# Gated projection weights built by GpSimd, products copied out by ScalarE, and a second LayerNorm in three groups

## What is computed

```
x = x + gate_msa[:, None, :] * _attention(_modulate(_layernorm(x), shift_msa, scale_msa), qkv_w, qkv_b, proj_w, proj_b)
x = x + gate_mlp[:, None, :] * _mlp(_modulate(_layernorm(x), shift_mlp, scale_mlp), fc1_w, fc1_b, fc2_w, fc2_b)
```

## Time and profile before

| | |
|---|---|
| median of 3 runs | 472.64 us |
| profiled execution, its own time | 472.34 us |
| its span (first to last instruction) | 470.6 us |
| TensorE busy | 429.0 us, 91% |
| VectorE busy | 287.5 us, 61% |
| ScalarE busy | 221.8 us, 47% |
| GpSimd busy | 89.2 us, 19% |
| mean granted TensorE clock | 0.964 of full speed |

### The profile page before, as it was taken

The page is one execution under the profiler, slowest core; times in us unless marked ns, Lnnn a source line. Parts: engine busy times, 40 slices in busy tenths (PEclk is TensorE's granted clock), DMA queues, the critical chain, the costliest instruction groups (busy, mean ns, idle before and its releaser), DMA issues.

```text
span 470.6 us, 11337 instructions
## 1 busy us (share of the span) xinstructions
PE 429.0 (91%) x4617; PEld 274.5 (58%) x4617; DVE 287.5 (61%) x808; ACT 221.8 (47%) x459; POOL 89.2 (19%) x108
## 2 busy tenths in 40 slices
PE   8999999999959999899968888877689999999987
PEld 4666655565636666666645665566434665656554
DVE  3698844576674644667737666567878555644422
ACT  3245533242037979687777677523256241421200
POOL 5059999950000000000000000013500000000000
PEclk9999999999979999899959899999969999999999
DMA  6996000000000000000000000000000000000011
GB/s 171 316 296 187 3 4 1 2 2 2 0 0 1 1 2 2 3 1 3 1 5 3 5 4 3 3 0 1 2 1 1 13 23 16 26 13 27 15 37 39
DMA packets 7785, 14.55 MB, mean 31 GB/s; under 512 B 2541, under 2 KB 6098, under 8 KB 7607
## 3 DMA queue, kind: packets, MB, share of 16 engines
q1 hardware_dynamic: 7732, 13.82, 9.8%
HBM read 11.37 MB, written 2.38 MB: 29 GB/s over the span
## 4 chain that ended last, share of the span: by engine, by line
PE 73%; DVE 12%; ACT 9%; issue 5%; ACTq 0%; DVEq 0%
PE psum L886 12%; PE psum L470 12%; PE psum L904 12%; PE psum L737 6%; PE psum L570 3%; DVE MX L1273 2%; PE psum L812 2%; PE psum L723 2%; ACT scratch L998 2%; PE psum L662 2%; PE psum L642 2%; ACT big L1030 2%; PE psum L582 2%; PE psum L687 2%; PE psum L526 1%
## 5 line engine op out<-in xcount | busy, mean ns | idle before, releaser
L886 PE MATMUL psum<-scratch,W 128*128 128x512 f16 (+1 forms) x252 | 60.9, 393 | 2.3 <-DVE scratch L1268 2.3
L470 PE MATMUL psum<-ident 128*128 128x320 f32 (+2 forms) x156 | 59.9, 472 | 0.0
L737 PE MATMUL psum<-WQ,scratch 128*128 128x288 f16 (+1 forms) x336 | 51.3, 297 | 5.0 <-DVE scratch L1279 5.0
L904 PE MATMUL psum<-W,big 128*128 128x288 f16 x432 | 55.7, 286 | 0.0
L464 POOL TENSOR_TENSOR X<-X,big 128x288 f32<-128x288 f32 x16 | 12.6, 794 | 225.4 <-DVE big L1388 224.2
L1108 ACT ACTIVATE big<-psum 128x512 f32<-128x512 f32 x36 | 21.5, 599 | 68.5 <-PE psum L886 68.4
L904 PEld LDWEIGHTS psum<-W,big 128*128 128x128 f16 x432 | 41.0, 98 | 13.7 <-issue 3.8
L1273 DVE TENSOR_REDUCE MX<-psum 128x8 f32<-128x1024 f32 x32 | 39.0, 1219 | 15.7 <-PE psum L687 15.2
L998 ACT ACTIVATE scratch<-psum,MOD 128x512 f32<-128x512 f32 (+3 forms) x48 | 34.2, 773 | 20.3 <-PE psum L662 7.3
L886 PEld LDWEIGHTS psum<-scratch,W 128*128 128x128 f16 (+1 forms) x252 | 25.3, 101 | 30.1 <-issue 3.7
L1412 DVE TENSOR_SCALAR big<-big 128x512 f16<-128x512 f32 x36 | 15.3, 424 | 44.1 <-ACT big L1108 44.0
(11 more groups left out here) (209 smaller groups left out, 767.3 us busy)
## 6 DMA issues: line engine op xcount, KB each, us to landing
X<-in_x_dram SPq DMA_DIRECT2D x4, 576.0 KB, 15.7
out_dram<-big SPq DMA_DIRECT2D x16, 144.0 KB, 1.7
big<-in_L_cond_W_dram SPq DMA_DIRECT2D x1, 2268.0 KB
big<-in_L_cond_ada_w_dram SPq DMA_DIRECT2D x2, 864.0 KB, 18.6
stage<-in_L_cond_fc_w_dram SPq DMA_DIRECT2D x1, 1296.0 KB
big<-in_L_cond_fc_w_dram SPq DMA_DIRECT2D x1, 1152.0 KB
stage<-in_L_cond_qkv_w_dram SPq DMA_DIRECT2D x1, 864.0 KB
big<-in_L_cond_fc_w_dram SPq DMA_DIRECT2D x3, 144.0 KB
```

The source lines that it names most:

```text
L470: pe.matmul(out[:, 0:cols], left, left[:, 0:1].broadcast_to([P, cols]), start=True, stop=True)
L737: mm = pe.matmul(UB[gu % 2][:, 0:D], HT[0:r, n % 2, a_, P * a:P * a + P], WQ[0:r, w_, D * w:D * w + D], start=(p_ == 0), stop=(p_ == 6))
L886: mm = pe.matmul(FB[idx % 3], W1[0:r, w_, P * m:P * m + P], HT[0:r, n % 2, a_, :], start=(p_ == 0), stop=(p_ == 6))
L904: mm = pe.matmul(YB[t % 2][:, 0:D], g[:, a_, f, cols], W2[:, w_, f, :], start=False, stop=(f == NF - 1 and w_ == 1))
```

## The change

1. GpSimd no longer prepares WP at the start. After its other preparations it waits for the attention gates and then, for each batch, multiplies the staged weights and bias by the gate and splits the product into halves (7 instructions per batch, semaphore `folded`). WP holds two batches. The attention gates go to GATE0, scaled by FINE.
2. ScalarE copies the projection's products out of PSUM (`product_out`), VectorE no longer does. The first PSUM bank of the three is bank 7 instead of bank 2.
3. The second LayerNorm is three groups: tiles 0 to 3, 4 to 7, 8 to 15. The variance step is a function of its own, `norm_var`. The first two groups' square roots lie among the projection's copies on ScalarE, the third in `gelu(9)` before m = 2. VectorE's statistics of tiles 8 to 11 lie in the first fc1 chunk, those of tiles 12 to 15 and `source(10)` in the second.
4. TensorE turns chunk 8 before it projects chunk 7, not after.

```diff
-        GATE = sb("GATE", [P, 2, B, D])
+        GATE = sb("GATE", [P, B, D])
...
-        QB = [bank[2], bank[5], bank[6]]
+        QB = [bank[7], bank[5], bank[6]]
...
-        NORMS = [(0, TPC * n, TPC) for n in range(NCH)] + [(1, 8 * b, 8) for b in range(B)]
+        NORMS = [(0, TPC * n, TPC) for n in range(NCH)] + [(1, 0, TPC), (1, TPC, TPC), (1, 8, 8)]
...
-            for src, dst, n, s_ in ((SWQ, WQ, 3 * D, in_wq), (SWP, WP, D, in_wp), (SW1, W1, MLP, in_w1)):
+            for src, dst, n, s_ in ((SWQ, WQ, 3 * D, in_wq), (SW1, W1, MLP, in_w1)):
...
+            pool.wait_ge(in_wp, 96)
+            pool.wait_ge(fill_done, FG + 3)
+            for b in range(B):
+                r = slice(0, 98)
+                chain(pool.tensor_tensor(WPG[:, 0:2, :], SWP[:, 0:2, :], GATE0[:, b, :].unsqueeze(1).broadcast_to([P, 2, D]), ALU.mult))
+                chain(pool.tensor_copy(WP[:, b, 0:2, :], WPG[:, 0:2, :]))
+                pool.tensor_tensor(WP[:, b, 2:4, :], WPG[:, 0:2, :], WP[:, b, 0:2, :], ALU.subtract).then_inc(folded, 1)
+                chain(pool.tensor_tensor(WPG[r, 2, :], SWP[r, 2, :], GATE0[r, b, :], ALU.mult))
+                chain(pool.tensor_copy(WP[r, b, 4, :], WPG[r, 2, :]))
+                chain(pool.tensor_scalar(WP[r, b, 4, :], WP[r, b, 4, :], lowrow[r, :], None, ALU.mult))
+                pool.tensor_tensor(WP[r, b, 4, :], WPG[r, 2, :], WP[r, b, 4, :], ALU.add).then_inc(folded, 1)
+                pool.wait_ge(folded, 2 * b + 2)
...
             turn(NCH)
             for n in range(NCH, 2 * NCH):
-                if n + 1 < 2 * NCH:
-                    turn(n + 1)
+                turn(n + 1)
                 project(n)
-            turn(2 * NCH)
...
+                    act.wait_ge(folded, 2 * B)
...
+            def product_out(t):
+                act.wait_ge(proj_ready, t + 1)
+                if t >= 6:
+                    act.wait_ge(x_mid, t - 5)
+                act.mul(YT[:, t % 6, :], QB[t % 3][:, 0:D], 1.0 / (FINE * FINE)).then_inc(proj_mul, 1)
+
             turn_out(NCH, None)
             for n in range(NCH, 2 * NCH):
-                if n + 1 < 2 * NCH:
-                    turn_out(n + 1, None)
-            norm_root(NCH)
-            turn_out(2 * NCH, 1)
-            norm_root(NCH + 1)
+                turn_out(n + 1, None if n + 1 < 2 * NCH else 1)
+                for j in range(TPC):
+                    product_out(TPC * (n - NCH) + j)
+                if n in (NCH + 1, NCH + 2):
+                    norm_root(n - 1)
...
+                    if n == 2 * NCH + 1 and m == 2:
+                        norm_root(NCH + 2)
...
+            def middle(t0, k):
+                for t in range(t0, t0 + k):
+                    dve.wait_ge(x_mid, t + 1)
+                    stat(1, t)
+
             split(NCH)
-            for n in range(NCH, 2 * NCH):
...
+            split(NCH + 1)
+            split(NCH + 2)
+            middle(0, TPC)
+            norm_var(NCH)
+            split(NCH + 3)
+            norm_scales(NCH)
+            source(2 * NCH, 1)
+            middle(TPC, TPC)
+            norm_var(NCH + 1)
             split(2 * NCH)
-            for t in range(NT - 3, NT):
-                dve.wait_ge(x_mid, t + 1)
-                stat(1, t)
+            norm_scales(NCH + 1)
             source(2 * NCH + 1, 1)
-            norm_scales(NCH + 1)
...
+                    if c_ == 1 and m == 2:
+                        norm_scales(NCH + 2)
+                        source(n + 1, 1)
...
+                    if c_ == 0 and m in FC2_AT:
+                        middle(8 + FC2_AT.index(m), 1)
+                    if c_ == 1 and m < 2:
+                        middle(12 + 2 * m, 2)
+                    if c_ == 1 and m == 1:
+                        norm_var(NCH + 2)
```

More of the change, by code:

```diff
@@ L53, in build @@
         o += 18 * D
+        SW1 = big[:, o:o + 12 * D].rearrange("p (b n) -> p b n", b=3)
+        o += 12 * D
+        assert 8192 + 2048 <= o - 3 * D and 12288 + 2 * D <= o
         SWP = big[:, o:o + 3 * D].rearrange("p (b n) -> p b n", b=3)
         o += 3 * D
-        SW1 = big[:, o:o + 12 * D].rearrange("p (b n) -> p b n", b=3)
-        o += 12 * D
+        WPG = big[:, WTILES * D:(WTILES + 3) * D].rearrange("p (b n) -> p b n", b=3)
+        GATE0 = big[:, 12288:12288 + B * D].rearrange("p (b n) -> p b n", b=B)
         JUNK = big[0:WROWS, o:o + 4 * D].rearrange("p (a n) -> p a n", a=4)
@@ L188, in build @@
         weights = sem("weights")
+        folded = sem("folded")
         mod_part = sem("mod_part")
@@ L856, in project @@
                 if n == NCH:
-                    pe.wait_ge(weights, 4)
+                    pe.wait_ge(folded, 2 * B)
                 for j in range(TPC):
@@ L862, in project @@
                     for p_, (a_, w_, r) in enumerate(PARTS):
-                        mm = pe.matmul(QB[t % 3][:, 0:D], HT[0:r, n % 2, a_, P * j:P * j + P], WP[0:r, w_, :], start=(p_ == 0), stop=(p_ == 6))
+                        mm = pe.matmul(QB[t % 3][:, 0:D], HT[0:r, n % 2, a_, P * j:P * j + P], WP[0:r, t // 8, w_, :], start=(p_ == 0), stop=(p_ == 6))
                     mm.then_inc(proj_ready, 1)
@@ L875, in fc1 @@
                 if n == 2 * NCH:
-                    pe.wait_ge(weights, 6)
+                    pe.wait_ge(weights, 4)
                 for m in range(NF):
@@ L893, in fc2 @@
                 if c_ == 0:
-                    pe.wait_ge(weights, 8)
+                    pe.wait_ge(weights, 6)
                 g = GT[c_ % 2]
@@ L921, in fill_out @@
                     g, b = divmod(n - FG - 1, 2)
-                    cp = act.mul(GATE[:, g, b, :], f[:, 0:D], 1.0 / (FINE * FINE))
+                    if n == FG + 1:
+                        act.wait_ge(weights, 4)
+                    cp = act.mul(GATE[:, b, :], f[:, 0:D], 1.0 / (FINE * FINE)) if g else act.mul(GATE0[:, b, :], f[:, 0:D], FINE)
                 elif work[n] == "P'":
@@ L1222, in stat, with norm_var @@
                 dve.bn_aggr(MV[:, l, t, :], BN[:, t % 2, :]).then_inc(bn_s, 1)
+            def norm_var(q):
+                l, t0, k = NORMS[q]
+                dve.wait_ge(bn_s, 2 * (NT * l + t0 + k))
+                dve.tensor_scalar(ST[:, l, 0, t0:t0 + k], MV[:, l, t0:t0 + k, 1], EPS, None, ALU.add).then_inc(stats, 1)
             def norm_scales(q):
@@ L1295, in _ @@
                 rotated(t)
+            norm_var(0)
             norm_scales(0)
@@ L1304, in _ @@
             ones_rows(0)
+            norm_var(1)
             norm_scales(1)
@@ L1342, in normalise @@
                 if w == 0:
-                    dve.wait_ge(weights, 8)
+                    dve.wait_ge(weights, 6)
                 for c_ in range(2):
```

26 lines of the change are left out of this document (5 added, 21 removed).

## The result

The changed kernel takes 475.30 us (475.38 as the median of all its 5 runs); the kernel before took 472.64 us beside it. The ratio is 1.0044, with a 95% interval of 1.0025 to 1.0062: slower by about 2.1 us, where I had forecast 1.1 us less. Times here are medians of the fast runs; of every kernel, the one before included, other executions are 6 to 16 us longer, and a few of those that count as fast lie about 5 us above the rest, which widens the intervals. Measured again as `again`, the changed kernel took 476.25 us beside 472.70 for the kernel before, 3.6 us more (ratio 1.0089, 1.0041 to 1.0137).

A forecast was written before the change was run, and what follows sets the result against it. TensorE, busy nine tenths and carrying the chain for most of the span, was taken as the bound. fc1's earlier start -2.86, clock 0, fc1(9) wait +1.7 gave -1.1 us: 471.5, stated as 471.4, range 468.4 to 474.5.

The forecast's parts named there:

- The fold: GpSimd's gate multiplication during QKV, about 145 to 159 us: covered, taken as 0, bounds 0 to 1.65 us.
- Products to ScalarE: In the projection, sixteen ScalarE copies of 0.41 us add nothing, and TensorE's 1.20 us pause goes.
- turn(7): Third block waits for the Sqrt table load and root: a 2.4 us pause, block 1.0 us later than before.
- VectorE's own line: From the block's split through norm_scales(4), 1.0 us, and source(8), 1.44, chunk 8 is ready at 332.6 us.
- The third block of turn(8): ScalarE takes the second root before turn_out(8), so TensorE pauses a new 3.35 us, 333.55 to 336.9.
- The clock: One fall again, over project(7) and perhaps fc1's start, priced 2.98 us as before: difference 0, bounds -3.0 to +2.0.
- my own pair of pauses: TensorE pauses of 0.6 and 3.35 us around turn(8), 0.9 us of work between, expected to bring the clock's fall.
- The third group: Inside fc1(9), statistics, root and source(10) make TensorE wait a new 1.7 us before chunk 10.
- The rivals: Clock holds, 468.5 us, chance 0.13; earlier fall, 0.19; fold holds VectorE, 0.12; Sqrt load before products, 0.03.
- B: Clock already falls in the pause stretched by the Sqrt load, 324.95 to 327.4 us: +1.9, 474.5 us, chance 0.19.

The follow-up runs named there:

- nofold: The changed kernel with the fold's 14 instructions at the start, ones in the gate's place; 476.45 us, ratio to the kernel before 1.0074.
- noadd: The changed kernel with GpSimd's 16 adds into X replaced by one-column memsets; 472.98 us, ratio to the kernel before 1.0003.
- rootlate: The changed kernel with the second root behind turn_out(8) on ScalarE instead of ahead of it; 473.41 us, ratio to the kernel before 0.9996.
- preload: The changed kernel with a one-column Sqrt after turn_out(5), loading the table while ScalarE is idle; 474.13 us, ratio to the kernel before 1.0029.
- fill: The changed kernel with dummy matmuls on TensorE ahead of its waits; 472.35 us, ratio to the kernel before 1.0006.
- rootstats: The changed kernel with the second root behind turn_out(8) and the third group's statistics, root and source(10) earlier; 471.00 us, ratio 0.9974.

## Why the prediction was wrong

**The fold.** Right. It is covered; the splits were held for 0.55 us each, inside my 0 to 1.65, and nothing remained (nofold).

**Products to ScalarE.** Right: the copies took 0.41 us, and the wait of 1.20 us went.

**turn(7).** Right: 2.35 us against the forecast 2.4, table load included. The root begins at 325.98, where the load begun at 324.69 has ended, so here too no drain shows beside the 1.28.

**VectorE's own line: the first step that failed.** I wrote "norm_scales(4) ... = 1.0; source(8), 1.44" from rows that stood alone. In the changed order the factors and the start of source(8) lie beside GpSimd's adds of chunk 6, and took 2.6 and 2.0 us; the wait before turn(8), 0.6 by my sum, was 2.88. I had the effect in hand, the 0.28 us step, and asked it only of the fold. noadd shows it: 0.68 us without the adds. The Trainium skill, "SBUF — State Buffer", Who interferes with whom, has the rule: a VectorE instruction with two SBUF inputs contends with a GpSimd instruction that reads SBUF, and a copy or tensor_scalar can contend in a mode that takes both ports, where whoever issues second is blocked for the whole instruction. The trace agrees for two inputs, with 0.16 against 0.54 and 0.69 us for such a step, while the reciprocal at 342.38, one input, kept its 0.18 us inside an add. The tensor_scalar steps were held too (0.66 against 0.17 us, and source(8)); in which mode they ran, no row shows. The term was mis-sized by about 2.2 us, and fc1's start came out at -1.3 with the clock held, where I had said -2.86.

**The third block of turn(8).** The mechanism was right, the second root holds turn_out(8); 2.99 us where I had 3.35.

**The clock: the second step that failed.** I set one fall against one fall, "so the difference is 0". There were three. One came over project(7), as said, and cost it 1.6 us and the block ahead of it 0.4, so less than the 2.98 of before. But the clock fell only 0.3 us into that pause, behind the 2.88 us that I had put at 0.6, and in rootlate it fell before the pause began. In noadd, where the first pause was 0.68 us, it fell late in the 2.99 (a granted clock of 0.87 in 335 to 336 us). So my own pair of pauses brings a fall too, but in `again` another was ahead of it. The other two I gave no chance: behind the wait before chunk 10, of which I had said only that TensorE waits (1.8 us), and before the last fc2 (1.7 us), where a wait that was there before, 1.88 us, was survived at 452 and not at 454. Why it was not survived in the changed kernel is not shown: the same wait is in both kernels, and noadd, rootlate and preload survived it in their profiled executions. fill shows the price of the three together, 5.1 us.

**The third group.** Right in kind and nearly in size: 1.94 us against 1.7; with the clock it cost 3.7.

**The rivals.** None came out as told. B had a fall in the Sqrt load's pause; the clock held there. Its sum, +1.9, is near the measured +2.1, by other falls. The measured medians, 475.3 and 476.25 us, lie above my range of 468.4 to 474.5: its upper end held one more fall, and no term for a source(8) that comes late.

## What to carry to other kernels

Where a change moves VectorE steps in time, price them beside what GpSimd does then, not from rows in which they stood alone; a step of 0.16 us can become one of 0.7. Count every TensorE wait, old ones too, as a possible fall of the clock, and test by filling the waits with dummy matmuls in both kernels: this parts the waits (+0.5 to +1.4 us here) from the clock (+2.1 to +3.1). Look for what a wait hides: with the clock held the kernel before met a GELU wait of 0.59 us, and with fc1 started sooner VectorE held fc1(8) for 1.86 us. When a scale has been folded into weights, see if the product still needs a copy: here PSUM could be added straight into its sum, and with the roots, statistics and dummy matmuls set right around it, 6 to 7.6 us were won.

## What the runs showed that I had not expected

The length of a pause did not order the falls. In `again` the clock held through 2.35 us before 327.45 and 2.88 us before 334.96, fell as the 2.99 us that came next began, and fell behind 1.94 us that followed unbroken work; the wait of 1.88 us before the last fc2 was survived in the kernel before and not in `again`. What turns a survived wait into a fall stays open.

The price of a fall differs as well. project(7) took 5.16 us in `again`, 5.88 in rootlate and 6.12 in noadd, where it began sooner after the fall: of 1.9 and 2.2 us of waits removed, 1.1 and 1.2 reached fc1. But this is no rule: in rootstats, with rootlate's short wait, it took 4.52, as the clock was back at full by 340 us (0.72 in 339 to 340), 2.3 us after project(7) began; in rootlate that took 4.7 us (0.71 in 348 to 349).
